# Half of a block's one-hots moved into the wait for x2's deviation, and the addition of b_fc moved forward, in a fused graph layer and slice attention

## The reference

```
xn  = layernorm(x)
agg = segment_sum(xn[src], dst, 6250)
h   = relu(agg @ W_rel + b_rel + xn @ W_root)                   # 512 wide
i, f, g, o = split(h @ W_ih.T + b_ih + b_hh)                    # f is not used
c   = sigmoid(i) * tanh(g);  hl = sigmoid(o) * tanh(c)
x   = x + hl @ W_fc + b_fc                                      # called xin, then res
x2  = layernorm(x)
sw  = softmax(((x2 @ W_x + b_x) @ W_slice + b_slice) / temp)     # per head, 8 heads of 64 slices
tok = sum over nodes of fx * sw;  a small attention over the 64 slice tokens of a head
out = x + (sw @ attended tokens) @ W_out + b_out
```

## Time and profile before

| | |
|---|---|
| Median of 3 runs | 1237.53 us (1236.96 to 1239.23) |
| The profiled execution, device time | 1240.34 us |
| Its span, first to last instruction | 1238.5 us |
| PE busy | 1116.1 us (90%) |
| DVE busy | 831.8 us (67%) |
| POOL busy | 805.3 us (65%) |
| ACT busy | 627.2 us (51%) |
| Mean granted TensorE clock | 0.994 of full speed |

### The profile page before, as it was taken

One profiled execution on the slowest core, in us unless ns is written; L12 is line 12 of the kernel. 1 busy time (PEld: TensorE's weight loads), 2 busy tenths in 40 slices (PEclk: granted clock), 3 DMA queues, 4 the chain that ended last, 5 costly groups with the idle time before them and its releaser, 6 DMA issues. The chain is left out here.

```text
span 1238.5 us, 30254 instructions
## 1 busy us (share of the span) xinstructions
PE 1116.1 (90%) x9821; PEld 967.1 (78%) x9821; DVE 831.8 (67%) x2560; ACT 627.2 (51%) x1257; POOL 805.3 (65%) x856
## 2 busy tenths in 40 slices
PE   1077799999999999999999999999999999999998
PEld 0046688878888888788888787888888878897798
DVE  7885476667666766676677756775767566746665
ACT  5872444554456454545554545455545454555332
POOL 5877777777777777777777777777777777400000
PEclk9998999999999999999999999999999999999999
DMA  8674444444454445444544444444444454313498
GB/s 313 225 268 119 125 130 136 147 142 136 129 148 142 141 124 150 140 140 123 150 149 138 121 148 150 137 121 150 147 136 122 150 149 137 97 44 116 129 336 290
DMA packets 92966, 188.74 MB, mean 152 GB/s; under 512 B 20914, under 2 KB 55591, under 8 KB 92821
## 3 DMA queue, kind: packets, MB, share of 16 engines
q0 software_dynamic: 39168, 107.01, 30.0%
q1 hardware_dynamic: 42794, 59.89, 14.8%
q10 hardware_dynamic: 10859, 20.05, 4.5%
HBM read 154.87 MB, written 32.00 MB: 151 GB/s over the span
## 5 line engine op out<-in xcount | busy, mean ns | idle before, releaser
L700 POOL DMA_INDIRECT ring<-table,sidx x798 | 763.5, 957 | 247.5 <-issue 242.7
L419 PE MATMUL ps<-h_h,wih_h 128*128 128x250 f32 x1200 | 338.8, 282 | 0.0
L420 PE MATMUL ps<-h_l,wih_h 128*128 128x250 f32 x1200 | 336.5, 280 | 0.0
L421 PE MATMUL ps<-h_h,wih_l 128*128 128x250 f32 x1200 | 336.5, 280 | 0.0
L419 PEld LDWEIGHTS ps<-h_h,wih_h 128*128 128x128 f32 x1200 | 230.1, 192 | 2.0 <-issue 0.8
L420 PEld LDWEIGHTS ps<-h_l,wih_h 128*128 128x128 f32 x1200 | 230.2, 192 | 1.1
L421 PEld LDWEIGHTS ps<-h_h,wih_l 128*128 128x128 f32 x1200 | 230.1, 192 | 0.0
L850 ACT ACTIVATE gate<-ps,bgate 128x250 f32<-128x250 f32 x300 | 124.2, 467 | 140.7 <-PE ps L421 139.7
L651 DVE TENSOR_SCALAR oneh<-iota,didx 128x64 f16<-128x64 f16 (+2 forms) x1179 | 183.1, 259 | 0.0
L1078 PE MATMUL ps<-ring,oneh 128*32 128x512 f16 x2280 | 151.0, 391 | 34.5 <-DMA ring<-table,sidx 31.9
L1078 PEld LDWEIGHTS ps<-ring,oneh 128*32 128x32 f16 x2280 | 59.5, 97 | 107.7 <-DMA ring<-table,sidx 46.4
(11 more groups left out here) (213 smaller groups left out, 2508.4 us busy)
## 6 DMA issues: line engine op xcount, KB each, us to landing
sp_ring<-table SPq DMA_DIRECT2D x1920, 1.0 KB
ring<-table,sidx POOLq DMA_INDIRECT x798
swt_d<-swt ACTq DMA_DIRECT2D x25, 500.0 KB
gate<-swt_d SPq DMA_DIRECT2D x19, 500.0 KB, 5.9
x_room<-in_x SPq DMA_DIRECT2D x12, 512.0 KB, 10.6
xn<-table SPq DMA_DIRECT2D x25, 224.0 KB
xin<-in_x SPq DMA_DIRECT2D x25, 224.0 KB
res<-xin SPq DMA_DIRECT2D x25, 224.0 KB
```

Of the source, the lines that this page charges most:

```text
L419: eng.matmul(dst, wh, xh, start=first, stop=False)
L420: eng.matmul(dst, wh, xl, start=False, stop=False)
L421: return eng.matmul(dst, wl, xh, start=False, stop=last)
L700: pool.indirect_dma_start(ring[:, j, :], None, table, bass.IndirectOffsetOnAxis(ap=idx, axis=0)).then_inc(done, 16)
```

## The change

`hots` gets a third parameter. With part 0 it waits for the buffer and writes the first half of the chunks' one-hots, with part 1 it writes the rest and raises `hot_done`, without it all is as before. VectorE's `norm_x2` ends behind `bn_aggr`, and what followed (the wait for the square root, rstd, nmr) becomes `scale_x2`. In a turn with `ffn` and `gather` VectorE now runs `norm_x2(t-2)`, `hots(2t, 1)`, `scale_x2(t-2)`. At the place where the whole of `hots(2t+2)` stood, it writes the first half only (turn 0 leaves its function before that place and writes the whole of block 2). `add_bfc(t-1)` moves from behind `cell_o(t-1, 3)` to behind `hots(2t+1)`, ahead of `cell_c(t-1, 0)`.

```diff
--- before.py
+++ after.py
@@ -642,15 +642,19 @@
                               ALU.subtract).then_inc(ln_lo[q], 1)
 
 
-        def hots(eng, b):
+        def hots(eng, b, part=None):
 
             e, (plan, _) = b % 2, hot_plan(b)
-            after(eng, sum_done[e], b // 2)
-            for j, (w0, w1, at) in plan.items():
+            half = len(plan) // 2
+            chunks = list(plan.items())[(part or 0) * half:half if part == 0 else len(plan)]
+            if part != 1:
+                after(eng, sum_done[e], b // 2)
+            for j, (w0, w1, at) in chunks:
                 n = WIN * (w1 - w0)
                 last = eng.tensor_scalar(oneh[:, e, at:at + n], iota[:, WIN * w0:WIN * w1], didx[:, j:j + 1],
                                          -float(WN * b), ALU.subtract, ALU.is_equal)
-            last.then_inc(hot_done[e], 1)
+            if part != 0:
+                last.then_inc(hot_done[e], 1)
 
 
         @block.gpsimd
@@ -1543,6 +1547,7 @@
                 dve.sem_inc(go, 1)
                 for e in range(2):
                     dve.bn_aggr(mv[0:WN, 0, e, :], stats[0:WN, 0, e, :]).then_inc(var_done, 1)
+            def scale_x2(p):
                 dve.wait_ge(sd_done, p + 1)
                 dve.reciprocal(rstd[0:WN, 0, 0:2], sd[0:WN, 0, 0:2]).then_inc(rstd_done, 1)
                 dve.wait_ge(rstd_done, 2 * p + 1)
@@ -1667,6 +1672,9 @@
                     low_rest()
                 if ffn:
                     norm_x2(t - 2)
+                    if gather:
+                        hots(dve, 2 * t, 1)
+                    scale_x2(t - 2)
                     if not gnn:
                         dve.wait_ge(att_pe, P_WT)
                         att_step(dve.tensor_copy(wqkvt, ps[0:D, HA, 0:3 * D].rearrange("p (k n) -> p k n", k=3)))
@@ -1680,6 +1688,8 @@
                 if gather and gnn:
                     hots(dve, 2 * t + 1)
                 if gnn:
+                    add_bfc(t - 1)
+                if gnn:
                     cell_c(t - 1, 0)
                     cell_o(t - 1, 0)
                 if gather:
@@ -1689,7 +1699,7 @@
                 if gnn:
                     cell_c(t - 1, 1)
                 if ahead:
-                    hots(dve, 2 * t + 2)
+                    hots(dve, 2 * t + 2, 0 if t else None)
                 if ffn:
                     softmax_end(t - 2)
                 if gnn:
@@ -1707,8 +1717,6 @@
                     cell_o(t - 1, 2)
                     cell_c(t - 1, 3)
                     cell_o(t - 1, 3)
-                if gnn:
-                    add_bfc(t - 1)
                 if gather:
                     add_halves(t, 1)
                 if gnn:
```

## The result

The changed kernel takes 1247.83 us (median of 6 runs, 1246.67 to 1250.11); the kernel before took 1237.37 us beside it. The ratio is **1.0083 (95%: 1.0070 to 1.0096)**. It is slower, and the time lies outside the range forecast. Of the kernels run later that compute the whole, one beats the kernel before, at 0.9982 (0.9972 to 0.9993): the kernel before with two more chunks given from GpSimd to SyncE. One run of the kernel "Spin" took 1633.21 us at a granted clock of 0.673 and is left out of its median and ratio.

What follows compares the result with a forecast made beforehand. GpSimd's back-to-back gather issue was taken to set the time up to 1056.2 us, TensorE's chain the rest. Terms 0 - 0.1 + 0 + 0 = -0.1 us took the median 1237.5 to 1237.4 us; range 1234.4 to 1241.2 us.

Steps and rivals of the forecast that it cites:

- The rate of GpSimd: Gathers stretched by VectorE operations: about the same number of hits by chance, so 0, with some 2 us either way.
- Rival B: More gathers stretched by VectorE, 0.18 us each; one more in each of 22 turns makes 4.0 us: 1241.5 us. Chance 0.13.
- Their last rows land when they did: In long turns the next block's sums start 0.68 us sooner, but its last gathered rows land unchanged; term 0.
- Behind the last wait: Behind 1056.2 us TensorE waits twice more for the weights, 1.3 us, in turns without one-hots; term 0.
- The wait that moves with b_fc: VectorE's `add_bfc` now waits for x sooner after its load's issue: a stall of 0 to 0.3 us, taken as 0.
- GpSimd's issue is the bound: Gathers go out back to back, one each 1.25 us, and set the time up to 1056.2 us.
- The wait for the weights: TensorE's wait ahead of the weight transposes, 0.68 us a turn, should go in all 22 turns: 15.0 us idle; term 0.
- The one-hots fit the hole: 12 one-hots, 1.8 us, go into VectorE's 4.01 us wait for the square root, which shrinks to about 2.2.
- The short turns: Turns with fewer gathers, where TensorE sets the pace: 39.94 us before, forecast to become 39.3.
- the long ones: Turns with 33 gathers, paced by GpSimd's issue, should keep 41.3 us.
- Rival A: TensorE is the bound, so the 15.0 us could come off: 1222.5 us. Chance 0.09.
- Rival C: x lands late, VectorE's first cell product 4 us late: 1 us and more in 22 turns, 1260 us. Chance 0.03.

Runs made afterwards that it cites:

- Spin: The changed kernel with 8 dummy matmuls on TensorE ahead of the wait for the last rows of each turn's first block: 1.0051, 1243.93 us.
- after: The changed kernel, its rows from one profiled execution of 1248.34 us; median 1247.83 us, 1.0083 against the kernel before.
- `add_bfc` alone: The kernel before with only `add_bfc` moved behind `hots(2t+1)`: 1.0053, 1245.09 us.
- one place later: The changed kernel with `add_bfc(t - 1)` behind `cell_o(t - 1, 0)`, one cell product and one cell output further on: 1.0016.
- b_fc in PSUM: The changed kernel without `add_bfc`; `norm_x2` adds b_fc to the output layer's PSUM in an operation with one SBUF input: 1.0010.
- one input: The changed kernel with the second operand left out of `add_bfc`, cell products, cell outputs and low parts of hl and x2: 0.9983, 1236.85 us.
- the one-hots alone: The changed kernel with `add_bfc` back in its old place, so only the one-hots are moved: 1.0022, 1241.35 us.
- Late x: The kernel with only the one-hots moved, and the load of x held back until the first block's sum is done: 1.0007.
- the fourth group: Every eighth gather left out (700 instead of 798) of the kernel before, the change, and only the one-hots moved: 1204.0, 1188.6 and 1179.9 us.
- the two chunks: The kernel before with 17 instead of 15 chunks brought by SyncE, at other places in the list, so 796 gathers: 0.9982.
- All together: Only the one-hots moved, x loaded behind the first block's sum, eight dummy matmuls, and 17 chunks from SyncE, against the kernel before: 0.9993, 1236.95 us.

## Why the prediction was wrong

**The step that failed** is the last term of the sum, "The rate of GpSimd": "I expect about the same number of hits by chance, so 0, with some 2 us either way." It was +7.7 us, 68 stretched gathers for 45; with it the run of gathers grew by 7.1 us. Its bound, 8.6 us "as much again", held, but I took the middle and a narrow band around it, and gave the range 3 us below and 4 above. Two things were wrong in it. The hits are not by chance alone: in turns paced by gathers VectorE stands at a fixed distance from GpSimd's starts, so a place is hit again and again: in after, the low parts of hl are hit in 23 turns. And a hit's price was taken from one row, 0.18 us, where those at `add_bfc` cost 0.50 each (6.0 / 12), up to 0.66 us of the pair's 0.75. Rival B named the mechanism and the side, but its one more hit a turn at 0.18 us made 4.0 us, half of what came. The row at 572.66 had shown the rule (it ends 0.82 us behind the operation's end), and I had not gone on to ask what a pair of 0.8 us would do. What no row of before could show is that the place behind the one-hots is the worse one: there no operation with two SBUF inputs had stood. Shown by: `add_bfc` alone (1.0053), one place later or in PSUM (1.0016, 1.0010), one input (0.9983). Which places are hit in a given order was not foreseeable from a row, and in that part the size is luck: with the one-hots alone the other places came to 9.3 us of stretching, with `add_bfc` one place later to 13.2 in all.

The Trainium skill (SBUF — State Buffer, section "Who interferes with whom") infers that descriptor generation on GpSimd is not held up by VectorE's two-input operations. The runs disagree for these gathers: 6.0 us of holding at the pair's new place, and a loss that goes when the second inputs go. The same section says that such an operation does contend with a GpSimd instruction that reads SBUF, and a gather takes its row numbers from `sidx`, which lies in SBUF. So I was wrong to write that by the page this rival would be worth 0: its first half may well cover a gather, and the trace agrees with that half (67 of 68 stretched gathers end a fixed 0.82 us behind a VectorE operation's end); no run here tells whether the reading of `sidx` is what waits. I had kept rival B against that sentence, and it should have had more.

**"Their last rows land when they did"** was out by 1.1 us: the flight itself grew, 3.89 for 2.78. The load of x waits for the high part of x2 (`x2_hi`), which TensorE's earlier stages now bring sooner against GpSimd, and so it goes out 0.6 instead of 2.5 us behind the gather. I had counted that load only as something waited for, not as traffic. Late x supports this; two profiles speak against a strict rule, as told there.

**Behind the last wait** I took 0. TensorE stood 3.9 us in one piece, then ran 3.4 us at half its clock (1.2 GHz), and the stretch took 1.3 us more. Idle time gathered in one wait was a risk that I did not price. The same fall came five times between 160 us and there, and GpSimd set the pace there.

**The wait that moves with b_fc**: 0 to 0.3 us in the steady turns held, but I had looked at turns from 130 us on. In turn 1 it was 9.56 us:

```profile
121.90 0.76 DVE L1534 TENSOR_TENSOR xin<-xin,bfc 125x256 f32<-125x256 f32 x2 [9.56 <-DMA xin<-in_x]
```

TensorE then waited 2.1 us for a gate. GpSimd's issue went on and set the time anyway; with an eighth of the gathers left out this place does cost, as told with the fourth group.

**What was right.** GpSimd's issue is the bound: two gathers fewer, 2.2 us less; an eighth fewer, and TensorE takes over. The wait for the weights went in all turns and came back as waits for rows: here is the gain that doesn't show. The one-hots fit the hole: the wait for the square root shrank from 4.01 to 2.24, as forecast to about 2.2:

```profile
560.95 0.17 DVE L1552 RECIPROCAL rstd<-sd 125x2 f32<-125x2 f32 x1 [2.24 <-ACT sd L821]
```

The short turns take 38.73 us, not the 39.3 forecast, for the reason told with the fourth group. And the long ones did not keep their 41.3 us: what TensorE gains in a short turn it waits for in the next, so the pair below takes 43.60 + 38.73 = 82.33 us, where the earlier trace rows has 41.37 + 39.94 = 81.31. A long turn and a short one:

```profile
547.43:591.03 43.60, 40.70 (x359) 35.73 (x358) 27.79 (x92) 21.02 (x45) 33.24 (x35) 0.96 0.46 135
591.03:629.76 38.73, 38.73 (x360) 34.18 (x359) 27.96 (x93) 21.11 (x45) 29.27 (x32) 1.00 0.48 141
```

Rival A is refuted for this kernel (its waits for gathers of "only 1 to 2 us" were read too low, by the way: the earlier trace rows has one of 3.0). Its size, 15.0 us, is about what the change brings once GpSimd is out of the way (15.4), but by luck: there the one-hots bring 24.1 and `add_bfc` takes 8.7 back. Rival C is refuted in the steady turns.

**Open.** Why the place behind the one-hots holds a gather longest, and what in a gather it is that waits. And the counts of stretched gathers are of one execution each: b_fc in PSUM, one place later and late x have 12.1, 13.2 and 10.0 us of it on their chip, where the two chunks, nearly the kernel before, have 11.8; of the kernel before itself I have no profile there. That the ratios follow the stretching within a chip is seen; that it explains each to the last microsecond is not.

## What to carry to other kernels

When an engine issues back to back and sets the time, an edit elsewhere is worth what it does to that engine's rate and to nothing else: list what runs beside it in the new order, and price a bad place by the length of what runs there, not by the one hit that the old order happens to show. A wait taken off an engine that is not the bound is not money saved but a reserve; it pays only with the edit that relieves the bound (here gathers left out: 24 us from the same one-hots), and gathered in one place it can even cost, by the clock (here 1.3 us). And read the first turns apart: their loads stand behind others' in the queue.

## What the hardware showed that I had not expected

- A stretched gather ends 0.82 us behind the end of a VectorE operation: 67 of 68 in after, 44 of 45 before. Its price is what that operation still had to run, less 0.13 us: at most 0.28 us in the single operations of 0.42 us in the steady turns of both.
- In after, a gather that begins right behind the one-hots in the pair of additions ends 0.82 us behind the pair, whether it began 0.03 us ahead of it or 0.57 us into it. Two operations further on, or with a gap of 0.08 us behind the one-hots (one gather), it ends 0.82 us behind the first addition.
- f16 one-hots themselves hardly hold gathers: of the 124 of after that began among them, at least 0.4 us ahead of their end, 108 took under 0.96 us and the longest 1.00. Operations on PSUM don't: 187 gathers, none over 0.96 us.
- What a gather costs GpSimd hardly hangs on its rows: 918 ns for 64, 969 for 128 in the same kernel.
- SyncE's queue goes over an edge: 17 chunks gained 2.2 us, and 18, with other edits beside them, lost 29 (0.9993 with 17 in the kernel "All together", 1.0235 with 18).
